# A two-layer tower on Trainium2: the expert products of the first layer as six fp16 products per tile

## The reference, cut to what matters

```python
def _L0_ffn_ref(x, W1, b1, Wg, bg, Wd, bd):        # C = 64, HID = 256, E = 8
    xf = x.reshape(-1, orig_shape[-1])
    H = jax.nn.gelu(xf @ W1 + b1, approximate=False)
    probs = jax.nn.softmax((H @ Wg + bg) / TEMP, axis=-1)
    assign = jnp.argmax(probs, axis=-1)
    out = jnp.zeros_like(xf)
    for e in range(Wd.shape[0]):
        y = H @ Wd[e] + bd[e]
        sel = (assign == e)[:, None]
        out = out + jnp.where(sel, probs[:, e:e + 1] * y, 0.0)
    return out.reshape(orig_shape)
...
h = _L0_tok_ref(...)
h = h + _L0_attn_ref(_layernorm(h, axis=-1), ...)
h = h + _L0_ffn_ref(_layernorm(h, axis=-1), ...)
h = h + _L1_attn_ref(_layernorm(h, axis=-1), ...)
h = h + _L1_ffn_ref(_layernorm(h, axis=-1), ...)
```

## Time and profile before

| | |
|---|---|
| median of the runs | 4984.24 us |
| span of the profiled execution | 4982.3 us (no other time is given for it) |
| PE busy | 4651.3 us, 93% |
| DVE busy | 3648.7 us, 73% |
| ACT busy | 3173.7 us, 64% |
| POOL busy | 2208.7 us, 44% |
| setup | up to 66.5 us |
| head of layer0 | 66.5 to 119.9 us |
| seven rounds of layer0 | 119.9 to 642.9 us |
| tail of layer0 | 642.9 to about 695 us |
| everything after | about 695 to 4982.3 us |

### The profile page before, as it was taken

How to read it: one execution, slowest core, us unless ns; L and a number is a source line. 1 busy time by engine, 2 the same in 40 slices (tenths; PEclk the granted TensorE clock), 3 DMA queues, 4 the chain that set the end, 5 groups by cost and what they waited for, 6 DMA issues and landing times. The chain is left out here.

```text
span 4982.3 us, 122822 instructions
## 1 busy us (share of the span) xinstructions
PE 4651.3 (93%) x42323; PEld 2070.5 (42%) x42323; DVE 3648.7 (73%) x6356; ACT 3173.7 (64%) x3464; POOL 2208.7 (44%) x2149
## 2 busy tenths in 40 slices
PE   5999979999999999999999979999999999999965
PEld 3444423333333333333333334444444444444433
DVE  4666656666666666666666678888888888888878
ACT  2443426666666666666666648888888888888844
POOL 2233243333332323233333346566666666666656
PEclk9999989999999999999999979999999999999966
DMA  4211100000000000000000000000000000000001
GB/s 101 68 51 51 51 1 2 1 2 1 2 1 2 1 2 1 2 1 2 1 2 1 1 1 3 3 3 3 3 3 3 3 3 3 3 3 3 3 7 27
DMA packets 43766, 52.86 MB, mean 11 GB/s; under 512 B 33416, under 2 KB 33544, under 8 KB 43144
## 3 DMA queue, kind: packets, MB, share of 16 engines
q1 hardware_dynamic: 40440, 44.03, 3.4%
q10 hardware_dynamic: 2704, 0.72, 0.1%
HBM read 39.73 MB, written 4.19 MB: 9 GB/s over the span
## 5 line engine op out<-in xcount | busy, mean ns | idle before, releaser
L1686 DVE TENSOR_REDUCE a_mp<-psum 128x1 f32<-128x512 f32 x2072 | 1325.2, 686 | 674.3 <-PE psum L1563 669.9
L2412 DVE TENSOR_REDUCE f_mp<-psum 128x1 f32<-128x512 f32 (+2 forms) x2352 | 1475.3, 684 | 212.8 <-PE psum L2234 200.0
L1531 ACT ACTIVATE a_prob<-psum,escale 128x1024 f32<-128x1024 f32 x1024 | 1087.0, 1110 | 534.3 <-PE psum L1612 533.9
L2194 ACT ACTIVATE f_prob<-psum,escale_f 128x1024 f32<-128x1024 f32 x1152 | 1247.4, 1112 | 226.2 <-PE psum L2303 109.9
L1620 PE MATMUL psum<-a_prob,a_v 128*64 128x512 f32 x4104 | 993.9, 605 | 0.0
L2048 POOL TENSOR_SCALAR f_hi<-f_raw,part 128x512 f16<-128x512 f32 x324 | 506.5, 1563 | 418.1 <-ACT f_raw L2152 411.8
L2234 PE MATMUL psum<-f_kf,f_qf 64*128 64x512 f16 (+2 forms) x3658 | 657.7, 309 | 35.5 <-DVE f_mp L2412 24.8
L1451 POOL TENSOR_TENSOR a_u<-a_og,a_inv 128x512 f32<-128x512 f32 x129 | 134.4, 1042 | 1166.1 <-DVE a_inv L1701 1166.1
L2324 PE MATMUL psum<-f_prob,f_vh 128*32 128x512 f32 (+3 forms) x6144 | 614.7, 495 | 6.3 <-DVE f_oc L2434 5.6
L2303 PE MATMUL psum<-f_qf,f_kf 64*128 64x512 f16 (+3 forms) x3074 | 505.6, 329 | 39.9 <-ACT f_og L2157 18.2
L1620 PEld LDWEIGHTS psum<-a_prob,a_v 128*64 128x64 f32 x4104 | 248.9, 136 | 504.9 <-issue 498.7
(11 more groups left out here) (440 smaller groups left out, 6749.0 us busy)
## 6 DMA issues: line engine op xcount, KB each, us to landing
idx<-in_itok_BS_dram SPq DMA_DIRECT2D x36, 512.0 KB, 6.3
idx<-in_itok_BS_dram SPq DMA_DIRECT2D x54, 256.0 KB, 7.6
idx<-in_x_dram SPq DMA_DIRECT2D x18, 256.0 KB, 3.7
a_qh<-a_rowT SPq DMA_DIRECT2D x258, 1.0 KB
out_dram<-h SPq DMA_DIRECT2D x16, 256.0 KB, 2.6
f_qf<-f_rowT SPq DMA_DIRECT2D x130, 4.0 KB, 1.7
wd<-in_L_ffn_Wd_dram SPq DMA_DIRECT2D x2, 256.0 KB
bd<-in_L_ffn_bd_dram ACTq DMA_DIRECT2D x16, 2.0 KB
```

The source lines that it names most:

```text
L1531: act.activation(prob[:, part], k.psum[:, pair:pair + 2].rearrange("p b n -> p (b n)"), ACT.Exp, scale=k.escale[:]).then_inc(s.read, 1)
L1686: dve.tensor_reduce(mp[:, tg % 2, t + 4 * r, c:c + 1], bank_of(j + r), X, ALU.max)\
L2194: act.activation(prob[:, u % NPF], k.psum[:, pair:pair + 2], ACT.Exp, scale=k.escale_f[:])\
L2412: dve.tensor_reduce(side[:, at[0]:at[-1] + 1:step], bank_of(j + r)[:, 0:len(at) * width].rearrange("p (a b) -> p a b", b=width), X, ALU.ma ...
```

## The change

The activations `hT` and the weights `wd` are each split into a high fp16 part and a low fp16 part (the rest after the high part). A tile's product is then the sum of three fp16 products per half: low activations x high weights, high x low, high x high; the fourth (low x low) is left out. So a tile has six fp16 products of 512 columns in place of two fp32 ones.

The weights are split once, at the end of `setup`, on GpSimd. The fp32 weights move to the memory that is free after setup, and the two fp16 copies live through layer0. The activations are split by GpSimd in `layer0`, two tiles at a time, by the new function `parted(pair, m)`: a copy to fp16 (128 x 512) and a subtraction (128 x 512). I write P0 to P7 for these. `hhi` and `hlo` have two sides, used in turn, so P(m+2) waits until the products of tiles 2m and 2m+1 are done (`y`). In GpSimd's list the order is P0 P1 | P2 S0 | P3 S1 | P4 S2 | P5 S3 | P6 S4 | P7 S5 | S6 | S7. PE waits for the split (`hlo`) ahead of every even tile.

```diff
@@ setup, gpsimd
             signal(ins, "ones_set")
+            wd = k.wd[:].rearrange("p a e c -> p a (e c)")
+            need(pool, "ones_set")
+            signal(pool.tensor_copy(k.wdhi[:], wd), "wd_hi")
+            need(pool, "wd_hi")
+            signal(pool.tensor_tensor(k.wdlo[:], wd, k.wdhi[:], ALU.subtract), "wd_lo")
@@ layer0
-        rs = sb("l0_rs", [P, 2, HALF], F32)
+        rs = sb("l0_rs", [P, 2, HALF // 2], F32)
+        hhi = sb("l0_hhi", [P, 2, 2, 2 * P], FP16)
+        hlo = sb("l0_hlo", [P, 2, 2, 2 * P], FP16)
@@ layer0, gpsimd
+                def parted(pair, m):
+
+                    j, at, side = m // 4, slice((m % 4) * 2 * P, (m % 4 + 1) * 2 * P), m % 2
+                    if m % 4 == 0:
+                        passed(pool, k.seen, E["gelu"], pair * 4 + 2 + j + 1)
+                    if m > 1:
+                        passed(pool, k.seen, E["y"], pair * 16 + 2 * m - 2)
+                    pool.tensor_copy(hhi[:, side], hT[:, j, :, at]).then_inc(E["hhi"], 1)
+                    passed(pool, k.seen, E["hhi"], pair * 8 + m + 1)
+                    pool.tensor_tensor(hlo[:, side], hT[:, j, :, at], hhi[:, side], ALU.subtract).then_inc(E["hlo"], 1)
+
                 def back(pair):
 
+                    for m in range(2):
+                        parted(pair, m)
                     for m in range(8):
+                        if m < 6:
+                            parted(pair, m + 2)
                         sums(pair, m)
...
+                pool.sem_inc(E["hlo"], 8)
@@ layer0, scalar, hidden
                     done("hid", pair * 4 + 2 * c + j + 1)
+                    done("hlo", pair * 8 + 4 * j + 4)
@@ layer0, tensor, experts
+                    if n % 2 == 0:
+                        done("hlo", pair * 8 + n // 2 + 9)
                     bank = ps[6 + n % 2]
+                    side, tokens = n // 2 % 2, slice(n % 2 * P, (n % 2 + 1) * P)
                     for c in range(2):
-                        last = pe.matmul(bank, lhsT=hT[:, j, c, t * P:(t + 1) * P], rhs=k.wd[:, c].rearrange("p e c -> p (e c)"),
-                                         start=(c == 0), stop=(c == 1))
+                        pe.matmul(bank, lhsT=hlo[:, side, c, tokens], rhs=k.wdhi[:, c], start=(c == 0), stop=False)
+                        pe.matmul(bank, lhsT=hhi[:, side, c, tokens], rhs=k.wdlo[:, c], start=False, stop=False)
+                        last = pe.matmul(bank, lhsT=hhi[:, side, c, tokens], rhs=k.wdhi[:, c], start=False, stop=(c == 1))
                     last.then_inc(E["y"], 1)
```

More of the change, by code:

```diff
@@ L66, in weight_loads @@
     k.bg = sb("bg", [P, EXPERTS], F32)
-    k.wd = sb("wd", [P, 2, EXPERTS, C], F32)
     k.rank = sb("rank", [P, EXPERTS], F32)
@@ L96, in weight_loads @@
     k.bias = k.early("bias", [P, 2, HALF], F32)
+    k.wdhi = k.early("wdhi", [P, 2, EXPERTS * C], FP16)
+    k.wdlo = k.early("wdlo", [P, 2, EXPERTS * C], FP16)
     tmp = k.tmp
@@ L137, in weight_loads @@
     k.fgn = tmp("fgn", [NH, 2, C], F32)
+    k.wd = tmp("wd", [P, 2, EXPERTS, C], F32)
     k.fg2 = tmp("fg2", [P, NH], F32)
@@ L321 @@
     pool=["clear", "consts", "max_all", "fc_twice", "spread0", "low00", "high00", "low01", "high01", "spread1", "low10", "high10", "low11", "high11", "hl_bias", "hl_rest", "mgate_ones",
-          "fmax_all", "ones_set"],
+          "fmax_all", "ones_set", "wd_hi", "wd_lo"],
 )
@@ L643 @@
             "vx", "kf", "qf", "ctx", "cx", "num", "den", "aT", "proj", "x2", "cen3", "sq3", "var3", "sd3", "xn3",
-            "hid", "gelu", "gate", "lg", "eg", "tr", "xt", "y", "y_taken", "pt", "tree", "h", "var4", "sd4", "gT", "gturn", "wsel", "wturn", "wT", "cc", "rs", "bc", "numS")
+            "hid", "gelu", "gate", "lg", "eg", "tr", "xt", "y", "y_taken", "pt", "tree", "h", "var4", "sd4", "gT", "gturn", "wsel", "wturn", "wT", "cc", "rs", "bc", "numS", "hhi", "hlo")
 class Link:
```

## The result

The changed kernel takes 5013.64 us (median of 4 runs, 5012.46 to 5019.57) against 4984.26 (the median of the four runs of the kernel before that were timed beside it). The ratio is 1.0058, with a 95% interval of 1.0045 to 1.0070. I had forecast 4970 and faster. The profiled execution spans 5012.4 us, 30.1 more than before.

What follows compares the result with a forecast made beforehand. PE was taken to set the pace of layer0's rounds. Setup +3.5, seven rounds -26.6 and tail +8.6 sum to -14.5 us on 4984.2, giving 4970 us, with an 8-in-10 range of 4955 to 4988.

Steps and rivals of the forecast that it cites:

- A tile's cost: Expert products in layer0: six fp16 products at 0.22 us make 1.32 us, saving 0.40 us per tile.
- A round, -3.8: Layer0's rounds: of at most 6.4 us saved on PE, 3.8 us kept per round, 26.6 over seven.
- GpSimd in a round: Layer0's rounds: split and sum take 5.67 us; GpSimd stays 0.4 us per unit short of being the bound.
- Rival A: Layer0's rounds: side chains shift with PE, so a round keeps 5.4 us; 4958.5 us in all, chance 0.12.
- rival B: Layer0's rounds and tail: dearer splits make GpSimd the bound, slower than before; 4991 us, chance 0.10.
- Rival C: VectorE's moments beside P0 and P1: GpSimd slows them, costing 2.7 us per round; 4988.6 us, chance 0.16.
- The tail, +8.6: End of layer0: GpSimd's splits and sums run without a gap and finish last, costing 8.6 us.
- The head, 0: Head of layer0, before the seven rounds: no change predicted, 0 us.
- Setup, +3.5: End of setup: the weights' cast and subtraction on GpSimd, with two waits, add 3.5 us, all on the path.

Runs made afterwards that it cites:

- the position restored: Changed kernel with 60 one-column matmuls that do no work (120 PE instructions) added in setup: 4977.05 us, ratio 0.9986.
- the run with one column: Changed kernel with 120 extra PE instructions in setup, weights split ahead of the second all-reduce, and GpSimd's activation splits cut to one column: 4970.73 us.
- the last version: Changed kernel with 120 extra PE instructions, weights split ahead of the second all-reduce, tail casts on ScalarE and subtractions on VectorE: 4965.13 us, ratio 0.9958.
- the early split: Changed kernel with GpSimd's split of the weights moved ahead of setup's second all-reduce: 5005.38 us, ratio 1.0035.

## Why the prediction was wrong

The step that failed is a zero in the sum that was not even written down. The sum 3.5 - 26.6 + 8.6 has terms for setup, the rounds and the tail, and none for what comes behind layer0: the code of attention1 and feedforward1 isn't touched ("Only the end of `setup` and `layer0` matter here"), so I took their time as fixed. I had counted the instructions that the change adds on PE for their duration and never for their place. That zero was +35.3 us, more than twice the whole forecast. None of the three rivals named it; all were about layer0. With the position restored the change gives 4977, and with the split of the weights moved as well 4975. The sign of the forecast is there, but that 4975 lies within 5 us of 4970 is in part luck: it is another kernel than the one forecast, and the feedforward alone differs by up to 16 us between kernels without a second standstill.

- **A tile's cost, 0.22 us per product:** right (0.217).
- **A round, -3.8:** right in kind, too small. The usual round went from 74.37 to 69.71, -4.66. The offsets from the round's start in the earlier trace rows and above give the steps. Up to the second context 39.74 against 39.41, so 0.33 kept (predicted 0.2). Up to the second spread of slot 6 52.05 against 50.36, 1.69 (1.4). Up to slot 9's variance 65.41 against 61.61, 3.80 (3.4). In slot 9 another 0.86 (0.4). Each small slack was a bit larger than I read from the waits. Two rounds of the seven are longer than the usual one in either of the two profiled executions, by 1.2 us before and by 2.4 and 1.3 after, which makes -31.3 out of 7 x -4.66; that I left open.
- **GpSimd in a round:** right. The unit is 5.38 against 5.67, since the next instruction starts 0.05 before the last one ends and the gap of 0.1 isn't there. The margin was real: rival B (GpSimd bound) is refuted by the run with one column.
- **Rival A (5.4 per round):** 4.66 is halfway to it. `kf` and the reciprocals did give way by a little.
- **Rival C (GpSimd in VectorE's way):** the effect came, the loss did not. These are the moments of the second batch in the round above, beside P0 and P1 (VectorE's timeline):

```profile
285.30 0.40 DVE L1163 TENSOR_SCALAR mean<-mean  x1
285.73 1.04 DVE L1164 TENSOR_TENSOR l_hc<-h,mean 128x512 f32 x1
286.81 1.53 DVE L1165 TENSOR_TENSOR l_hc<-l_hc 128x512 f32<-128x512 f32 x1
```

  The same three take 0.17, 0.69 and 0.69 for the first batch, and for both batches in the one-column kernel. So they lose 1.42 us a round, where the prediction had 4.0 for C against a slack of 1.30. The usual round is equally long (69.71) with the splits and without, so none of it reached the round's end.
- **The tail, +8.6:** right, +9.4. PE waits for `hlo` 8.6 us in all, and VectorE for `tree` 8.8.
- **The head, 0:** it was +2.9, but it isn't the change's. With one small instruction on GpSimd (73.5 us, above) the head takes 56.1, in the old kernel with 136 instructions more 56.2. In these and in the changed kernel PE's granted clock was 0.67 to 0.68 from 10 to 30 us into layer0, where the profiled execution of before had 0.66 and then 1.00. Where it was 0.66 and then 0.83 (112 instructions more, and the last version), the head took 53.3 and 53.5.
- **Setup, +3.5:** the term was mis-sized by the reload, 7.76. The two operations themselves were right. I had the rows of the durations, and took them from places where GpSimd had long been running such operations. The remaining 1.0 us is the second all-reduce, which came at 63.19 against 62.20.

## What to carry to other kernels

Code that is added anywhere moves every loop behind it in its engine's program. Before a result of half a per cent is believed, compare the blocks that the change doesn't touch, and if one of them differs, shift the program by a few dozen instructions that do no work and time again, looking at all loops, since a shift that frees one can catch another. On GpSimd, price an operation by what stood before it on the engine: here the first TENSOR_TENSOR behind an all-reduce waited some 7 us, and it should fall where the engine isn't awaited.

## What the runs showed of the hardware that I had not expected

- At every turn of the feedforward's loop PE stands still 2.8 to 3.4 us behind the branch in the kernels without a second standstill (in 2 to 5 of the 7 turns nothing shown ends it), and for up to 2.9 us a second time if, as inferred, a block's border lies just behind the target.
- A second standstill of 2.5 us goes with a loss of 5 us at a turn, and with a lower granted clock in the 10 us around it (0.59 against 0.83).
- The granted clock around a turn differs between kernels that have the same code there and no second standstill: 0.89 to 1.00 over 30 us, and 8 us of the feedforward's time.
- GpSimd's change of kind costs in the other direction too: the all-reduce behind the early split has 5.87 us of idle time before it that nothing shown ends.
